# A transformer layer with a mixture of experts: all task positions drawn anew, and ScalarE writes the second bf16 part of queries and keys

## What is computed

```
q, k, v = (split_heads(x @ W.T) for W in (Wq, Wk, Wv))
scores = where(causal, q @ k.T * 8 ** -0.5, -inf)
x1 = layernorm(x + merge_heads(softmax(scores) @ v) @ Wo.T)
s = sigmoid(x1 @ router_w.T)                  # 64 experts, top 4 of 8 groups, then top 8
coef = 2.5 * s[chosen] / sum(s[chosen])
h = silu(x1 @ Wg[e]) * (x1 @ Wu[e]) * coef[:, e]
y = layernorm(x1 + sum_e h @ Wd[e] + shared(x1))
```

## Time and profile before

| | |
|---|---|
| median of 3 runs | 962.25 us |
| the profiled execution, its own time | 962.95 us |
| span from its first to its last instruction | 961.2 us |
| TensorE (PE) busy | 940.5 us, 98% |
| VectorE (DVE) busy | 752.1 us, 78% |
| GpSimd (POOL) busy | 597.8 us, 62% |
| ScalarE (ACT) busy | 468.0 us, 49% |
| chain that ended last, PE's share | 85% |

### The profile page before, as it was taken

How to read it: one execution, slowest core, us unless ns; L and a number is a source line. 1 busy time by engine, 2 the same in 40 slices (tenths; PEclk the granted TensorE clock), 3 DMA queues, 4 the chain that set the end, 5 groups by cost and what they waited for, 6 DMA issues and landing times.

```text
span 961.2 us, 16058 instructions
## 1 busy us (share of the span) xinstructions
PE 940.5 (98%) x5012; PEld 574.7 (60%) x5012; DVE 752.1 (78%) x2374; ACT 468.0 (49%) x866; POOL 597.8 (62%) x651
## 2 busy tenths in 40 slices
PE   9899999999999999999999999999999999999996
PEld 4355466666666666666666656666666655666663
DVE  4776877799877997789967997789877997478655
ACT  2355445455555545555455545555455555543221
POOL 2343147765777757776766757776676767775653
PEclk9799999999999999999999999999999999999999
DMA  8551144432643253423633345323634223242431
GB/s 287 171 160 62 49 158 138 135 107 87 205 133 116 91 182 114 135 78 114 214 125 101 105 159 160 111 81 97 211 112 124 93 103 113 88 144 77 160 109 55
DMA packets 64340, 121.70 MB, mean 127 GB/s; under 512 B 6656, under 2 KB 36224, under 8 KB 63744
## 3 DMA queue, kind: packets, MB, share of 16 engines
q1 hardware_dynamic: 64256, 120.67, 39.1%
HBM read 98.37 MB, written 22.02 MB: 125 GB/s over the span
## 4 chain that ended last, share of the span: by engine, by line
PE 85%; DVE 7%; DMA 3%; issue 2%; POOL 1%; ACT 1%; SPq 0%; POOLq 0%; DVEq 0%
PE acc L844 12%; PE ob L785 7%; PE sm L755 7%; PE st L773 7%; PE pg L714 6%; PE pu L714 6%; PE pg L716 5%; PE pg L715 5%; PE pu L716 5%; PE pu L715 5%; PE acc L710 4%; PE acc L829 3%; PE acc L831 2%; PE acc L830 2%; PE ob L797 2%
## 5 line engine op out<-in xcount | busy, mean ns | idle before, releaser
L958 POOL TENSOR_TENSOR hid<-hid,coef_b 128x512 f32<-128x512 f32 x240 | 309.4, 1291 | 158.5 <-DVE hid L1215 99.6
L1147 DVE CUSTOM_DVE_ANT_0 max_out<-sm,causal_sb 128x128 bf16<-128x128 f32 (+3 forms) x512 | 236.0, 485 | 58.0 <-PE sm L755 54.0
L907 ACT ACTIVATE hid<-pg 128x512 f32<-128x512 f32 x243 | 145.4, 598 | 209.7 <-PE pg L716 203.4
L879 ACT ACTIVATE probs<-st 128x512 f32<-128x512 f32 (+1 forms) x384 | 194.5, 525 | 93.6 <-PE st L773 90.3
L1206 DVE SCALAR_TENSOR_TENSOR hid<-hid,pg 128x512 f32<-128x512 f32 x243 | 165.3, 680 | 54.4 <-ACT hid L907 53.2
L1215 DVE TENSOR_TENSOR hid<-hid,pu 128x512 f32<-128x512 f32 x235 | 160.3, 682 | 40.7 <-PE pu L716 37.9
L962 POOL TENSOR_TENSOR hid_lo<-hid,hid_hi 128x512 fp32r<-128x512 f32 x112 | 144.4, 1290 | 64.9 <-ACT hid_hi L914 64.3
L944 POOL TENSOR_SCALAR_AFFINE_SELECT probs<-probs 128x256 f32<-128x256 f32 x256 | 98.4, 410 | 61.5 <-ACT probs L879 61.5
L755 PE MATMUL sm<-k_stack,q_stack 72*128 72x128 bf16 (+3 forms) x512 | 132.5, 308 | 3.0 <-DMA k_stack<-k_rows_dram 2.4
L773 PE MATMUL st<-q_stack,k_stack 96*128 96x512 bf16 (+3 forms) x512 | 128.6, 304 | 0.1
L714 PE MATMUL pg<-x_hi,wg_hi 128*128 128x512 f32 x240 | 126.5, 527 | 1.3 <-DVE hid L1206 0.9
(11 more groups left out here) (161 smaller groups left out, 1295.5 us busy)
## 6 DMA issues: line engine op xcount, KB each, us to landing
coef_b<-coef_dram SPq DMA_DIRECT2D x128, 512.0 KB, 3.9
q_rows_dram<-qk_parts SPq DMA_DIRECT2D x24, 384.0 KB, 3.4
k_rows_dram<-qk_parts SPq DMA_DIRECT2D x24, 384.0 KB, 3.6
q_stack<-q_rows_dram SPq DMA_DIRECT2D x64, 144.0 KB
k_stack<-k_rows_dram SPq DMA_DIRECT2D x64, 144.0 KB
xT_sb<-in_xT SPq DMA_DIRECT2D x8, 256.0 KB, 3.9
y<-in_x SPq DMA_DIRECT2D x8, 256.0 KB, 4.2
out<-out_sb SPq DMA_DIRECT2D x8, 256.0 KB, 2.4
```

The costliest lines, as they stand in the source:

```text
L879: act.activation(probs[:, h % HG, at:at + wide], st_bank[i % 2][:, 0:wide], ACT.Exp, scale=C ** -0.5).then_inc(exp_done, 1)
L907: act.activation(hid_of(n, i), gate_bank(n, i)[:, :], ACT.Tanh, scale=0.5).then_inc(tanh_done, 1)
L958: pool.tensor_tensor(hid_of(n, i), hid_of(n, i), coef_b[:, half % 2, j, :], ALU.mult)\
L1147: last = dve.tensor_tensor_reduce(out=max_out[:, seg.nth(BANK_SM, task) % 2, col:col + wide], in0=sm_of(seg, task)[:, col:col + wide], in1 ...
```

## The change

Three things change. First, every position in all nine tables is a new number. Second, part 2 of queries and keys is written by ScalarE (a copy of the rest, rounded to bf16) instead of VectorE's TENSOR_REDUCE over one element; a new semaphore tells VectorE, whose part 3 then waits for ScalarE. Third, `rest` has a buffer for queries and one for keys, so that VectorE may form the rest of the keys before part 3 of the queries is done. The tables below are cut to one pair of lines; the code is whole.

```diff
 STEADY = {
-    "qsplit": (-63.926, -63.598,),
+    "qsplit": (-63.53979, -63.39836,),
...
-        rest = sb("rest", [P, S])
+        rest = sb("rest", [P, 2, S])
...
+        part2_done = sem("part2_done")
...
+                    if kind in ("qsplit", "ksplit") and i == 0:
+                        side = int(kind == "ksplit")
+                        after(act, seg, sm_free, BANK_SM, (kind[0], n, 0))
+                        act.activation(qk_parts[:, side, 1, :], rest[:, side, :], ACT.Copy).then_inc(part2_done, 1)
...
-                        bank_free(dve, seg, parts_done, ("q", "k"), task)
-                        dve.tensor_tensor(rest[:, :], sm_of(seg, task)[:, :], qk_parts[:, kind == "k", 0, :],
-                                          ALU.subtract).then_inc(sm_free, 1)
-                    if kind in ("qsplit", "ksplit"):
-                        parts = qk_parts[:, kind == "ksplit"]
-                        if i == 0:
-                            after(dve, seg, sm_free, BANK_SM, (kind[0], n, 0))
-                            done(dve.tensor_reduce(parts[:, 1, :], rest[:, :].unsqueeze(2), AX_X, ALU.max), kind)
-                        else:
-                            ready(kind)
-                            dve.tensor_tensor(parts[:, 2, :], rest[:, :], parts[:, 1, :], ALU.subtract)\
-                                .then_inc(parts_done, 1)
+                        bank_free(dve, seg, parts_done, ("q", "k"), task, banks=2)
+                        dve.tensor_tensor(rest[:, int(kind == "k"), :], sm_of(seg, task)[:, :],
+                                          qk_parts[:, kind == "k", 0, :], ALU.subtract).then_inc(sm_free, 1)
+                    if kind in ("qsplit", "ksplit") and i == 1:
+                        side = int(kind == "ksplit")
+                        dve.wait_ge(part2_done, 2 * n + side + 1)
+                        dve.tensor_tensor(qk_parts[:, side, 2, :], rest[:, side, :], qk_parts[:, side, 1, :],
+                                          ALU.subtract).then_inc(parts_done, 1)
```

More of the change, by code:

```diff
@@ L103 @@
[L103 to L111, removed]
+    "ld": (-76.7507,),
+    "q": (-50.93722,),
+    "qsplit": (-50.66079, -48.94697,),
+    "k": (-48.87715,),
@@ new lines @@
+    "ksplit": (-48.47927, -47.73467,),
[15 rows of a table added]
+    "mask": (-39.03992, -37.39484, -37.32583, -36.94273, -31.25913, -30.7338, -30.08023, -29.08557, -27.81986,
+        -26.66397, -26.36583, -25.19732, -20.78545, -20.24591, -19.88258, -19.72824,),
+    "pv": (-34.88723, -28.97451, -24.85882, -19.37186,),
+    "ot": (-33.27463, -25.65026, -23.12255, -18.05471,),
+    "on": (-29.90143, -25.13718, -19.62442, -18.04602,),
+    "ldtok": (-42.25458,),
+    "attT": (-17.7286,),
+    "oproj": (-17.32073,),
+    "ln": (-17.07762, -16.5355, -16.07172,),
@@ L112 @@
+    "x1": (-15.55211, -15.45216, -15.43766, -15.36331,),
+    "x1T": (-15.15932,),
+    "router": (-13.19709,),
+    "tk": (-12.65353, -11.79998, -11.7573, -11.16747, -10.71274, -10.43217, -10.04656, -9.41425, -9.07109,
+        -8.70075, -8.51231, -8.46499, -8.24867, -8.08777, -7.11391, -6.80736, -6.04407, -3.46561, -3.39453,
+        -3.31118,),
+    "coefT": (-1.08702,),
+    "c": (0.31178, 2.1134,),
 }
 SECOND = {
-    "ld": (-72.431,),
-    "q": (-71.761,),
-    "qsplit": (-69.767, -69.62,),
@@ L143 @@
[L143 to L148 removed]
+    "ld": (-73.79594,),
+    "q": (-69.04486,),
+    "qsplit": (-68.66368, -68.56373,),
+    "k": (-68.33498,),
+    "ksplit": (-67.79488, -67.59614,),
[16 rows of a table added]
+    "mask": (-49.56944, -48.88586, -48.52525, -45.10727, -39.53259, -38.54414, -36.53533, -32.7035, -25.01371,
+        -24.63173, -22.58164, -22.14261, -17.41764, -16.1384, -15.63222, -13.27709,),
@@ new lines @@
+    "pv": (-44.90295, -31.29579, -21.81224, -12.74874,),
+    "ot": (-43.17254, -29.06277, -19.55562, -11.55225,),
+    "on": (-40.72554, -21.94977, -14.81873, -10.79822,),
+    "ldtok": (-12.10603,),
+    "attT": (-9.5665,),
+    "oproj": (-9.31113,),
+    "ln": (-8.59766, -8.52312, -8.33507,),
+    "x1": (-8.24336, -8.14016, -8.03071, -7.79909,),
+    "x1T": (-7.03462,),
+    "router": (-6.27931,),
+    "tk": (-6.00089, -5.61305, -5.36058, -4.46755, -4.31948, -4.03995, -4.01819, -3.92627, -3.87342, -3.72926,
+        -3.07928, -2.98123, -2.93764, -2.35089, -1.86746, -1.622, -1.1494, -1.04391, -0.68312, -0.34765,),
@@ L175 @@
[L175 to L185 removed]
+    "ld": (-72.64358,),
+    "q": (-65.55209,),
+    "qsplit": (-65.05298, -64.19535,),
@@ new lines @@
+    "k": (-62.50278,),
+    "ksplit": (-60.61702, -59.80888,),
[14 rows of a table added]
+    "mask": (-42.33651, -42.014, -38.54562, -38.54368, -35.84722, -32.54332, -32.03785, -30.52961, -26.35399,
+        -25.92014, -25.58019, -22.60412, -19.24944, -16.57914, -14.93998, -14.29402,),
+    "pv": (-37.50514, -29.86813, -21.64387, -13.96744,),
+    "ot": (-35.97575, -28.29477, -19.06467, -12.08334,),
+    "on": (-35.54131, -21.69334, -17.25958, -10.72098,),
+    "ldtok": (-15.75247,),
+    "attT": (-9.68789,),
+    "oproj": (-9.25609,),
@@ L186 @@
+    "ln": (-9.10948, -8.8305, -8.64798,),
+    "x1": (-8.33928, -7.91404, -7.04669, -7.03104,),
+    "x1T": (-6.4881,),
+    "router": (-5.23271,),
+    "tk": (-4.8126, -4.72586, -4.68918, -4.54065, -4.47772, -4.42232, -4.37245, -4.16264, -3.94934, -3.93785,
+        -2.88377, -2.71506, -2.51908, -2.41415, -1.7989, -1.18049, -0.87096, -0.52153, -0.2783, -0.11999,),
+    "coefT": (0.70899,),
+    "c": (0.93334, 1.02101,),
 }
 STEADY = {
-    "ld": (-85.024,),
-    "q": (-64.276,),
-    "qsplit": (-63.926, -63.598,),
@@ new lines @@
+    "pv": (-37.13106, -29.65257, -21.45296, -13.66889,),
+    "ot": (-36.60995, -27.754, -18.27495, -12.08712,),
+    "on": (-36.24056, -25.97932, -15.03547, -10.23036,),
+    "ldtok": (-11.19142,),
+    "attT": (-9.83394,),
+    "oproj": (-9.21356,),
+    "ln": (-9.03805, -8.98291, -8.7871,),
+    "x1": (-8.25232, -7.77493, -7.30484, -7.17522,),
+    "x1T": (-6.49053,),
+    "router": (-5.66765,),
+    "tk": (-5.47949, -5.38842, -5.15663, -5.08333, -4.70332, -4.45947, -4.43236, -4.03075, -3.81736, -3.39613,
+        -3.27078, -2.98905, -2.8924, -2.37553, -2.21263, -1.75239, -1.24051, -1.11705, -0.72756, -0.44141,),
@@ L285 @@
+    "fin": (35.01461,),
+    "finT": (35.5641,),
+    "ln": {3: 36.01743, 4: 37.22987, 5: 37.34529},
+    "finx": (37.97447, 39.62519, 39.97289, 44.63445,),
 }
 EXPERTS = {
[25 rows of a table removed]
-    "fin": (35.023,),
-    "finT": (35.171,),
-    "ln": {3: 35.23, 4: 35.628, 5: 35.634},
-    "finx": (36.26, 37.209, 37.362, 41.234,),
[33 rows of a table added]
+    "fin": (35.15865,),
+    "finT": (35.57507,),
+    "ln": {3: 35.58765, 4: 35.82797, 5: 35.86676},
+    "finx": (37.10113, 37.68641, 37.85189, 41.76014,),
 }
 EXPERTS_LAST = {
[21 rows of a table removed]
-    "fin": (86.494,),
@@ L340 @@
-    "finT": (86.639,),
-    "ln": {3: 89.451, 4: 91.074, 5: 91.399},
-    "finx": (92.632, 93.567, 99.558, 104.396,),
[27 rows of a table added]
+    "fin": (96.40536,),
+    "finT": (96.753,),
+    "ln": {3: 97.1996, 4: 100.32142, 5: 102.93304},
+    "finx": (107.73017, 107.73913, 108.81745, 112.09071,),
 }
 WEIGHTS = {
-    "wld": (-56.531, -56.384, -47.421, -46.872, -42.585, -41.341, -40.132, -39.275, -25.529,),
-    "chunk": (-49.604, -47.209, -45.46, -44.958, -41.133, -40.296, -35.179, -34.642, -24.091,),
+    "wld": (-64.01188, -52.11215, -47.6205, -47.46299, -43.9597, -41.25746, -39.6625, -37.09062, -28.57236,),
@@ L347 @@
+    "chunk": (-56.67708, -47.11707, -46.76868, -44.70277, -41.27095, -41.0331, -35.30701, -33.30581,
+        -24.97616,),
 }
```

90 lines of the change are left out of this document (14 added, 76 removed), and 337 rows, old and new, of tables (EXPERTS, EXPERTS_FIRST, EXPERTS_LAST, EXPERTS_SECOND).

## The result

The changed kernel takes 956.74 us, the median of 13 runs (953.82 to 960.43); the kernel before took 963.02 us in the same rounds (13 runs). The ratio is 0.9937, 95% interval 0.9924 to 0.9950: 4.8 to 7.3 us faster. The forecast was 957.9 us, range 954.5 to 962.5. It held, but one of its terms, the new waits, hid two errors of about 3 us each in opposite directions, and the head went another way than forecast. As a difference, 4.35 us less were forecast (from 962.25) and 6.28 us less were measured (from 963.02).

A forecast was written before the change was run, and what follows sets the result against it. TensorE (PE), busy 98% of the span, was taken as the bound. Terms of -0.9, -4.3, -0.6, +1.0 and +0.4 sum to -4.4 us: 958.55 us profiled, 957.9 us as median, range 954.5 to 962.5 us.

The forecast's parts named there:

- the new waits: Expert chains at new distances: one more PE wait in the whole program, +0.4 us; ends -1.0 and +3.2 us.
- the head: Before the first `mT`: VectorE's first reads and the second stack load come later, so `mT` does too, +1.0 us.
- Cheaper neighbours: On TensorE: 71 fewer places with a 128-column piece right ahead of an expert product, 0.06 us each, -4.3 us.
- Fillers: Matmuls that nobody reads, filling up PE in the head: four fewer at 0.218 us each, -0.9 us.
- bf16 behind fp32r: On TensorE: 39 fewer places of bf16 right behind an fp32r product, 0.015 us each, -0.6 us.
- Part 2 on ScalarE: VectorE loses 10.8 us, ScalarE gains 9.6 us of copies; both lie beside TensorE, so costed at nothing.
- rival C: In the head the slow clock comes twice or covers 6.5 us more: +3.2 us, 961.1 us; chance 0.12.
- rival E: Slow clock stays away or falls before the first `mT`, where VectorE is the bound: -3.2 us, 954.7 us; chance 0.12.
- the steps of 0.3 us: Sign in the steady stretch: the 0.29 to 0.30 us steps between matmul ends would be gone.
- the half clock: Sign in the head: a granted clock of half beyond 43 us would show the forecast wrong.
- The bound of 4 us: Sign: waits of PE between 140 and 861 us summing to more than 4 us would show the forecast wrong.
- Two signs: In the steady batch: VectorE 1.3 us less busy and ScalarE 1.2 us more.

The follow-up runs named there:

- Run 1: Kernel before with only the two matmuls of the 384- and 128-column score piece swapped, 128 first: 960.60 us, ratio 0.9969.
- run 2: Kernel before, all positions kept, with only the code part (part 2 on ScalarE, two buffers for the rest): 962.80 us, ratio 0.9993.
- run 3: Changed kernel's positions with the old code (part 2 on VectorE, one buffer for the rest): 957.12 us, ratio 0.9938 to the kernel before.
- Run 4: Changed kernel with the split of chunk 0 moved back behind the keys' first part: 955.79 us, ratio 0.9930 to the kernel before.
- run 5: Changed kernel with all weights of the head back where they stood before: 958.17 us, ratio 0.9946 to the kernel before.
- run 9: Changed kernel with GpSimd's second split of a weight chunk in the head waiting for the first negated maxima: 956.30 us, ratio 0.9926.
- run 11: Changed kernel once more, unaltered: 957.24 us.
- the moved `mT`: Changed kernel with the fourth `mT` of batches 3 to 7 placed 0.28 units later: 957.00 us, ratio 0.9936 to the kernel before.

## Why the prediction was right, term by term

*Cheaper neighbours, forecast -4.3 us: right in mechanism, a little large.* Run 1 shows the price at 0.052 us a place: 71 x 0.052 = 3.7 us. The trace of the changed kernel has 8 such places between the routers of batches 1 and 7, that of before 73.

*Fillers, -0.9 us, and bf16 behind fp32r, -0.6 us:* 240 fillers, and 241 against 276 first and transposed scores in the same stretch; neither was tested by itself. In the trace of before the median step of a bf16 matmul is 0.180 us behind an fp32r product and 0.163 behind a bf16 matmul (384 columns), 0.233 and 0.218 (512 columns): the 0.015 of the prediction.

*Part 2 on ScalarE, 0 us: right,* by runs 2 and 3.

*New waits, forecast +0.4 us: two errors that cancelled.* The first is the wait ahead of the fourth `mT`. PE's steps into the `mT` tasks between the routers of batches 1 and 7 sum to 5.31 us, before to 2.45: +2.9 us. The prediction had +3.2 as its outer end, "one in each of 8 batches", and looked for it among the expert chains only. The second error is the sentence "Between 140 and 861 us PE stood idle for only 1.0 us". It took the view of waits for the time lost. That view counts idle time between the modelled end of one matmul and the start of the next, and a matmul normally starts some 0.16 us before the one ahead has ended. The kernel before, TensorE in order of time:

```profile
445.04 0.38 PE L755 MATMUL sm<-k_stack,q_stack 72*128 72x512 bf16 x1
445.49 0.50 PE L714 MATMUL pg<-x_hi,wg_hi 128*128 128x512 f32 x1
```

The score ends at 445.42, the gate product at 445.99: a step of 0.57 us where 0.23 is the rule, 0.34 us lost, and no wait is marked. Between the routers of batches 1 and 7 the kernel before had 26 first gate or up matmuls that took over 0.03 us more than 0.231 us, not counting those behind 128-column pieces and behind `pv`: 5.7 us over it together. The changed kernel has 15, 2.8 us over it. The new positions removed 2.9 us of such stalls, of which the view of waits shows 0.3 us, and the prediction did not see them. By chance it is what the `mT` cost, and so the sum came out right by luck.

*The sum of that stretch.* -3.4 (65 places), -0.5 (35 bf16 places), -2.9 and +2.9 make -3.9 us; measured are -3.1 us (from 209.38 to 859.39 us before, 210.40 to 857.32 after). Of the 0.8 us between, 0.6 lie in expert products right behind `pv`: there are 12 before and 15 after, and each takes some 0.20 us over the plain step (0.43 against 0.231 us for a gate or up product). The prediction has no term for this neighbour. The rest is open. Behind the last router another 0.5 us are won.

*The head, forecast +1.0 us: its mechanism failed, and its size is not shown.* The prediction said: "The stores ahead leave earlier". They left later: the first store of the queries' part 1 was issued at 8.34 us, before at 6.82, because chunk 0 stood ahead of the queries. The prediction looked at chunks 2 and 3 and did not see chunk 0. Run 4 shows its cost at the values, 1.56 us; run 5 shows that the moves of chunks 2 and 3, from which the +1.0 was worked out, do not set the head's end. In the profile the first `mT` came 3.7 us late and the router of batch 0 3.2 us. That is this execution's loss; the first `mT` came between 32.9 and 36.8 us over all kernels, the old positions with the new code (run 2) among the late ones with 36.7.

For the median there is an estimate. From the router of batch 0 on, the profiled executions with the old positions took 857.7 us of their own time (before) and 856.2 (run 2), those with the new ones behind the head 850.6 to 852.2 (the changed kernel and runs 3, 4, 5, 9 and 11). If the median runs took as long there, the changed kernel gets to that point between 2.2 us earlier and 0.8 us later than before; +1.0 us lies just outside. So most of the 6.3 us is won behind the head: 3.1 and 0.5 as above, and 2.1 between the routers of batches 0 and 1 (103.07 to 100.97 us). There stand 35 fillers instead of 40, 1.1 us by the prediction's 0.218 us each, and six of the 71 places, 0.3 us; the other 0.7 is open.

*The slow clock, rivals C and E.* The granted clock from 24 to 45 us was between 0.59 and 0.92 in the profiles of these kernels, and 0.59 twice with the changed positions. Heads that came out late mostly had a low clock there (run 5 did not: 35.89 us at 0.84); whether the clock makes the head late or a late head the clock was not settled.

*What would have shown it wrong:* the steps of 0.3 us are gone but for 8, the half clock ended at 42.3 us, the waits between 140 and 861 us sum to 3.8 us. The bound of 4 us was nearly met, and by a wait that the prediction had not named. Two signs came out otherwise: from router to router VectorE is busy 0.7 us less (91.28 to 90.58), not 1.3, and ScalarE as long as before (58.26 and 58.24), not 1.2 us more.

## What to carry to other kernels

Read the pace of a pipelined engine from end to end of its instructions, pair by pair, before you trust its list of waits: stalls of up to 0.37 us stood outside that list here, and the stalls ahead of gate and up products summed to 5.7 us where the list showed 1.0. When a position moves, go through every engine's list for what now stands ahead of an instruction that waits for a DMA; a small chunk ahead of the first real work held that work up here by up to 1.6 us. And a wait that is taken away at its victim can come back at the next one in line, as with the moved `mT`; move its source.
